# Attention scores from two products of 128 rows per sub-head, with keys stacked high and low and queries doubled, in place of three products of 64 rows

## The reference, cut to what matters

```
q, k, v = xn @ wq.T, xn @ wk.T, xn @ wv.T      # q, k: 8 heads x 2 sub-heads of 64; v: 8 heads of 64
scores  = q @ k.T / 8                          # for each of the 16 sub-heads, 1024 x 1024, causal
attn    = softmax(scores)                      # fp32
attn    = attn[first sub-head] - lmbda * attn[second sub-head]
out     = attn @ v                             # then a root-mean-square norm, and @ wo.T
```

## Time and profile before

| | |
|---|---|
| median of 3 runs | 3775.64 us (3774.65 to 3775.76) |
| the profiled execution | 3770.78 us |
| its span, first to last instruction | 3769.0 us |
| mean granted TensorE clock | 0.94 |
| PE busy | 3183.8 us, 84% |
| DVE / ACT / POOL busy | 1951.8 / 1364.2 / 1859.7 us |

### The profile page before, as it was taken

The page is one execution under the profiler, slowest core; times in us unless marked ns, Lnnn a source line. Parts: engine busy times, 40 slices in busy tenths (PEclk is TensorE's granted clock), DMA queues, the critical chain, the costliest instruction groups (busy, mean ns, idle before and its releaser), DMA issues. The chain is left out here.

```text
span 3769.0 us, 46728 instructions
## 1 busy us (share of the span) xinstructions
PE 3183.8 (84%) x16049; PEld 2443.1 (65%) x16049; DVE 1951.8 (52%) x3951; ACT 1364.2 (36%) x2989; POOL 1859.7 (49%) x1707
## 2 busy tenths in 40 slices
PE   2899999899999979999989999995888983088776
PEld 0677777677777767777767777773776762044443
DVE  6355556645565655655664556565544655811110
ACT  2344444344444424444443444443323321022221
POOL 3256667646576645765773657654222241033333
PEclk9899999999999999999999999997998986589998
DMA  5211111321111141110123111103121111099897
GB/s 156 83 37 43 40 37 43 106 71 45 31 43 45 40 134 40 40 48 29 40 84 98 43 37 40 42 21 121 54 70 67 58 64 60 18 266 246 240 245 177
DMA packets 251183, 301.99 MB, mean 80 GB/s; under 512 B 19664, under 2 KB 168016, under 8 KB 250320
## 3 DMA queue, kind: packets, MB, share of 16 engines
q1 hardware_dynamic: 236624, 263.49, 22.3%
q0 software_dynamic: 14336, 35.66, 4.5%
HBM read 233.46 MB, written 65.57 MB: 79 GB/s over the span
## 5 line engine op out<-in xcount | busy, mean ns | idle before, releaser
L799 ACT ACTIVATE probs<-score_ps,neg_max 128x640 f32<-128x640 f32 (+7 forms) x512 | 374.4, 738 | 363.0 <-DVE neg_max L660 362.5
L690 POOL TENSOR_TENSOR probs<-probs 128x512 f32<-128x512 f32 (+3 forms) x384 | 383.4, 1013 | 10.7
L685 POOL TENSOR_SCALAR probs<-probs,comb 128x512 f32<-128x512 f32 (+3 forms) x384 | 230.0, 607 | 309.2 <-DVE comb L596 301.3
L660 DVE TENSOR_REDUCE neg_max<-score_ps 128x2 f32<-128x256 f32 (+7 forms) x256 | 346.5, 1353 | 58.9 <-PE score_ps L915 55.2
L694 POOL TENSOR_TENSOR out_root<-out_root,neg_half 128x16 f32<-128x16 f32 x128 | 371.8, 2907 | 5.7 <-DVE out_root L630 5.7
L552 DVE TENSOR_TENSOR layer_sum<-product_ps,layer_sum 128x512 f32<-128x512 f32 x384 | 262.4, 684 | 44.7 <-PE product_ps L61 41.6
L912 PE MATMUL score_ps<-keys_all,queries_all 64*128 64x512 f32 (+3 forms) x2304 | 277.2, 363 | 0.0
L539 DVE TENSOR_TENSOR attT<-turn_ps,attT 128x512 fp32r<-128x512 f32 (+3 forms) x384 | 211.6, 551 | 84.5 <-ACT attT L720 84.3
L720 ACT ACTIVATE attT<-turn_ps 128x512 fp32r<-128x512 f32 (+3 forms) x384 | 188.2, 490 | 142.8 <-PE turn_ps L825 142.8
L912 PEld LDWEIGHTS score_ps<-keys_all,queries_all 64*128 64x128 f32 x2304 | 187.8, 185 | 74.0 <-issue 44.7
L59 PE MATMUL product_ps<-xT_hi,w_up 128*128 128x512 f32 x512 | 211.6, 413 | 28.3 <-DVE queries_all L559 20.2
(11 more groups left out here) (248 smaller groups left out, 7676.3 us busy)
## 6 DMA issues: line engine op xcount, KB each, us to landing
e_gate_up<-in_w_gate_dram SPq DMA_DIRECT2D x64, 384.0 KB, 4.0
e_gate_up<-in_w_up_dram SPq DMA_DIRECT2D x64, 384.0 KB, 5.4
e_down<-in_w_down_dram SPq DMA_DIRECT2D x64, 384.0 KB, 6.8
w_stage<-in_wqk_dram SPq DMA_DIRECT2D x64, 256.0 KB, 3.1
w_stage<-in_w1T_dram SPq DMA_DIRECT2D x64, 256.0 KB, 2.6
w_stage<-in_w3T_dram SPq DMA_DIRECT2D x64, 256.0 KB, 2.7
values_by_head<-hidden_split SPq DMA_DIRECT2D x32, 512.0 KB, 3.2
w_stage<-w_transformed SPq DMA_DIRECT2D x64, 256.0 KB, 2.7
```

The lines of the kernel that those rows point to most:

```text
L660: dve.tensor_reduce(nmax[:, i % 2, :], score_tile(i % NT), AX.X, ALU.max, negate=True)\
L685: pool.tensor_scalar(PR[:, r, 1, c], PR[:, r, 1, c], comb[:, i % 4:i % 4 + 1], 1.0, ALU.mult, ALU.mult)\
L690: pool.tensor_tensor(PR[:, r, 0, c], PR[:, r, 0, c], PR[:, r, 1, c], ALU.add).then_inc(s_comb, 1)
L799: act.activation(PR[:, i % 2, q, 0:(j + 1) * P], score_tile(j)[:, q, :], ACT.Exp, bias=nmax[:, i % 2, q:q + 1], accum_out=sums[:, i % 16, ...
```

## The change

K holds, per head and sub-head, 128 rows: the sub-head's 64 rows of high parts on one half of the partitions and its low parts on the other half. Q holds, per sub-head, the high and the low part of the queries, each on both halves of the partitions. A product of 128 rows then gives query part x (high key + low key) at once, and two of them (high and low query) make the scores of a sub-head; low x low, which was left out before, comes with it. So a chunk of keys takes 4 matmuls of 128 rows in place of 6 of 64.

`proj_high` and `proj_low` write each half of the partitions by an instruction of its own (64 rows each), since the halves go to different places. The other half of Q is filled by DMA, from SBUF to SBUF: `double_queries`, two transfers of 256 KB for each half of a head's tokens, issued by SP when `proj_low` has freed the bank; `scores` waits for them (semaphores z_q_double0 and z_q_double1) at j = 0 and j = 4.

Q has room for one head only. So the queries of a head are projected later (`proj_at`): quarters 0, 1 and 2 of head h+1 in steps 2, 4 and 6 of head h, and quarter 3 in step 0 of head h+1 itself. In slot 12 there are three quarters instead of four. The weights wv can no longer be put into Q during head 7: their four pieces move from steps 3 and 4 of head 7 to slots 0 and 1.

```diff
--- before.py
+++ after.py
@@ -278,6 +278,7 @@
         s_vld = [sem("z_v_load0"), sem("z_v_load1")]
         s_gbf, s_gbfree, s_ph, s_tanh = sem("z_gb_filled"), sem("z_gb_free"), sem("z_proj_high"), sem("z_tanh")
         s_hh, s_hl = sem("z_hidden_high"), sem("z_hidden_low")
+        s_qd = [sem("z_q_double0"), sem("z_q_double1")]
         s_scf, s_max, s_exp = sem("z_sc_filled"), sem("z_max"), sem("z_exp")
         s_rs, s_cc, s_scaled, s_comb = sem("z_recip"), sem("z_comb_factor"), sem("z_scaled"), sem("z_comb")
         s_ttf, s_tth, s_ttfree = sem("z_tt_filled"), sem("z_tt_high"), sem("z_tt_free")
@@ -311,7 +312,10 @@
 
         def proj_at(i):
 
-            return (i // NT + 1, i % NT // 2) if 0 <= i < STEPS - NT and i % 2 == 0 else None
+            if not 0 <= i < STEPS or i % 2:
+                return None
+            h, q = (i // NT, 3) if i % NT == 0 else (i // NT + 1, i % NT // 2 - 1)
+            return (h, q) if h < HEADS else None
 
         def pair_at(i):
 
@@ -328,6 +332,8 @@
                 got += {0: [("wv", 0, 0, 0), ("wv", 0, 1, 0)], 1: [("wv", 0, 2, 0), ("wv", 0, 3, 0)],
                         2: [("qk", 0, 0, 1)], 3: [("qk", 0, 0, 0)], 4: [("w1", 0, 0, 0)], 5: [("w3", 0, 0, 0)],
                         6: [("w1", 0, 0, 1)]}.get(s, [])
+            if hb and s in (0, 1):
+                got += [("wv", hb, 2 * s, 0), ("wv", hb, 2 * s + 1, 0)]
             if hb is not None and s == HEAD_SLOTS - 1:
                 got.append(("qk", hb, 1, 1))
             if b is not None and i < STEPS:
@@ -340,8 +346,6 @@
                     got.append(("qk", *after, 0))
                 if s8 in (1, 2):
                     got.append(("w2", b, 2 * h + s8 - 1, 0))
-                if s8 in (3, 4) and h == HEADS - 1 and more:
-                    got += [("wv", b + 1, 2 * (s8 - 3), 0), ("wv", b + 1, 2 * (s8 - 3) + 1, 0)]
                 if s8 == 5 and more:
                     got.append(("w1", *after, 0))
                 if s8 == 6 and more:
@@ -378,7 +382,7 @@
                 if pair_at(i):
                     gb["W", b, i] = len(gb)
             if hb is not None and s == HEAD_SLOTS - 1:
-                for q in range(4):
+                for q in range(3):
                     gb["P", hb, 0, q] = len(gb)
             for v in pieces_at(b, i, hb, s):
                 piece[v] = len(order)
@@ -410,6 +414,9 @@
 
         def wv_part(part):
             return (K, Q)[part][:, 0, :, :].rearrange("p a n -> p (a n)").rearrange("p (k n) -> p k n", k=KT)
+
+        def query_quarter(b, h, half):
+            return gb["P", b, h, 2 * half + 1] + 1, slice(half * D, (half + 1) * D)
 
         def place(part, v):
             kind, _, a, c = v
@@ -472,6 +479,13 @@
                 def load_values(b, h):
                     sp.dma_start(Vh[:, h % 2, :, :].rearrange("p t n -> p (t n)").bitcast(F32), v_d[b, h])\
                       .then_inc(s_vld[h % 2], 16)
+
+                def double_queries(b, h, half):
+                    done, c = query_quarter(b, h, half)
+                    sp.wait_ge(s_gbfree, done)
+                    for q, here, there in ((0, lo64, hi64), (1, hi64, lo64)):
+                        v = Q[:, q, :, c].bitcast(F32)
+                        sp.dma_start(v[there], v[here]).then_inc(s_qd[half], 16)
 
                 for t in range(2):
                     load_x(0, t)
@@ -512,6 +526,10 @@
                         h = (i + 5) // NT
                         sp.wait_ge(s_pvf, b * GROUPS + 4 * (h - 2) + 4)
                         load_values(b, h)
+                    if b is not None and i < STEPS and proj_at(i - 1) and proj_at(i - 1)[1] % 2:
+                        double_queries(b, proj_at(i - 1)[0], proj_at(i - 1)[1] // 2)
+                    if hb is not None and s == HEAD_SLOTS - 1:
+                        double_queries(hb, 0, 0)
                     for v in pieces_at(b, i, hb, s):
                         load_piece(piece[v] + 3)
                 for t in range(NT):
@@ -555,11 +573,14 @@
                 def proj_low(b, h, q):
                     c, r = slice(q // 2 * D, (q // 2 + 1) * D), h % 2
                     dve.wait_ge(s_ph, (b * HEADS + h) * 4 + q + 1)
-                    if q % 2:
-                        ins = dve.scalar_tensor_tensor(Q[:, r, 1, c], gbank("P", b, h, q), 0.125,
-                                                       Q[:, r, 0, c].bitcast(F32), ALU.mult, ALU.subtract)
-                    else:
-                        ins = dve.tensor_tensor(K[:, r, 1, c], gbank("P", b, h, q), K[:, r, 0, c].bitcast(F32), ALU.subtract)
+                    raw = gbank("P", b, h, q)
+                    for sub, here, there in ((0, lo64, hi64), (1, hi64, lo64)):
+                        if q % 2:
+                            ins = dve.scalar_tensor_tensor(Q[here, sub, 1, c], raw[here, :], 0.125, Q[here, sub, 0, c].bitcast(F32),
+                                                           ALU.mult, ALU.subtract)
+                        else:
+                            ins = dve.tensor_tensor(K[there, r, sub, c], raw[here, :], K[here, r, sub, c].bitcast(F32),
+                                                    ALU.subtract)
                     ins.then_inc(s_gbfree, 1)
 
                 for b, i, hb, s in phases():
@@ -730,10 +751,12 @@
                 def proj_high(b, h, q):
                     c, r = slice(q // 2 * D, (q // 2 + 1) * D), h % 2
                     act.wait_ge(s_gbf, gb["P", b, h, q] + 1)
-                    if q % 2:
-                        ins = act.activation(Q[:, r, 0, c], gbank("P", b, h, q), ACT.Copy, scale=0.125)
-                    else:
-                        ins = act.activation(K[:, r, 0, c], gbank("P", b, h, q), ACT.Copy)
+                    raw = gbank("P", b, h, q)
+                    for sub, here in ((0, lo64), (1, hi64)):
+                        if q % 2:
+                            ins = act.activation(Q[here, sub, 0, c], raw[here, :], ACT.Copy, scale=0.125)
+                        else:
+                            ins = act.activation(K[here, r, sub, c], raw[here, :], ACT.Copy)
                     ins.then_inc(s_ph, 1)
 
                 def piece_high(v):
@@ -743,7 +766,7 @@
                     if before in gb:
                         act.wait_ge(s_gbf, gb[before] + 1)
                     if v[0] == "wv" and v[1]:
-                        act.wait_ge(s_scf, (v[1] - 1) * STEPS + STEPS - NT)
+                        act.wait_ge(s_scf, v[1] * STEPS)
                     act.activation(place(0, v), staged(v), ACT.Copy).then_inc(s_wh, 1)
 
                 for b, i, hb, s in phases():
@@ -898,7 +921,8 @@
                     hd, j = divmod(i, NT)
                     n, r = (j + 1) * P, hd % 2
                     if j in (0, 4):
-                        pe.wait_ge(s_gbfree, gb["P", b, hd, 1 if j == 0 else 3] + 1)
+                        pe.wait_ge(s_gbfree, gb["P", b, hd, j // 2] + 1)
+                        pe.wait_ge(s_qd[j // 4], 32 * (b * HEADS + hd + 1))
                     done = b * STEPS + i - (1 if 1 <= j < 4 else 0)
                     if done:
                         pe.wait_ge(s_exp, 2 * done)
@@ -907,10 +931,10 @@
                         pe.wait_ge(s_vlo, (b + 1) * NT)
                     for c0 in range(0, n, D):
                         w = min(D, n - c0)
-                        for m, (qp, kp) in enumerate(((0, 0), (1, 0), (0, 1))):
-                            for q, rows in enumerate((lo64, hi64)):
-                                pe.matmul(score_bank(q, j, c0)[:, 0:w], Q[rows, r, qp, j * P:(j + 1) * P],
-                                          K[rows, r, kp, c0:c0 + w], start=(m == 0), stop=(m == 2 and c0 + w < n))
+                        for q in range(2):
+                            for part in range(2):
+                                pe.matmul(score_bank(q, j, c0)[:, 0:w], Q[:, q, part, j * P:(j + 1) * P],
+                                          K[:, r, q, c0:c0 + w], start=(part == 0), stop=(part == 1 and c0 + w < n))
                     for q in range(2):
                         ins = pe.matmul(score_bank(q, j, c0)[:, w - P:w], identb[:, :], mask[:, :], start=False, stop=True)
                     ins.then_inc(s_scf, 1)
```

## The result

| | before | after |
|---|---|---|
| median, same chip | 3775.14 us | 3938.32 us (3928.33 to 3941.26) |
| ratio, 95% interval | | 1.0441 [1.0424, 1.0458] |
| profiled execution, span | 3770.78, 3769.0 us | 3936.04, 3934.3 us |

The account below looks back on a forecast made before the run. The prediction took PE's own order in layer 0 as the bound: its score time and its waits. Terms of -11 + 55 + 16 + 2 + 2 + 7 = +71 us put the median at 3847 us, range 3812 to 3893.

Parts of the forecast that it names:

- B: Projection's readers at pair heads: two instructions each free the bank 1.14 us later, all on PE at 48 places; +55 us.
- C: Row maximum at j = 7: DVE runs without idle time, so the 1.14 us delay reaches PE's attT wait; +16 us.
- F: The clock: waits grown beyond 2.2 us halve the granted clock behind a quarter of 24, 1.2 us each; +7 us.
- A: Scores on PE: four full-height products per chunk replace six half-row ones, whose ends of 0.30 us per block vanish; -11 us.
- D: Start of a batch: PE reaches the first scores sooner and waits 0.6 us for the query copies, four times; +2 us.
- E: Pieces of wv moved to slots 0 and 1 on POOL: the next batch's first norm starts 0.9 us late, three times; +2 us.
- not slower: Rival: 64-row reader instructions take half the time of 128-row ones, so the readers cost nothing; 3768 us, chance 0.04.
- ends stay: Rival: the 0.30 us per score block is no matter of half rows and remains; 3924 us, chance 0.06.
- weights: Rival: weights no longer load under products, so each score product pays 185 ns; 4131 us, chance 0.01.
- copies late: Rival: SP reaches the query doubling so late that PE waits 1 us at each of 60; 3907 us, chance 0.03.
- waits absorbed: Rival: PE's other waits in the same step shrink by half of the readers' cost at pair heads; 3819 us, chance 0.09.

Follow-up runs that it names:

- b_split: Kernel before with only the projection's readers (proj_high on ACT, proj_low on DVE) split into two instructions of 64 rows each; 3926.2 us, 1.0417.
- b_scores: Kernel before with only the score products changed to two of full height per sub-head, on the old buffers (scores are other numbers); 3776.0 us, 1.0015.
- d_ms: b_split with one small DVE instruction, the mean square of out_root, moved to POOL; 3874.7 us, 1.0286 against before.
- b_ms: Kernel before with the small mean-square instruction on out_root moved from DVE to POOL; 3770.3 us, 1.0002.
- b_sched: Kernel before with only the moved steps: projection quarters one slot later, wv's pieces in slots 0 and 1; 3771.1 us, 1.0002.
- c_fill: b_split with groups of 18 small bf16 products added on PE in its waits, results unused; 3877.6 us, 1.0279 against before.
- c_dve: Kernel before with only DVE's half of the reader split (proj_low in two 64-row instructions, proj_high whole); 3839.7 us, 1.0178.
- c_act: Kernel before with only ACT's half of the reader split (proj_high in two 64-row instructions, proj_low whole); 3804.7 us, 1.0094.
- a_pipe: Changed kernel with ACT signalling after each 64-row instruction and DVE waiting only for the one it needs; 3849.0 us, 1.0200 against before.

## Why the prediction was wrong, by its own steps

The readers were priced at 78 us and cost 157. Of b_split's 153.5 us in the steps, B has 62 (forecast 55), C's three steps 24 (16 with step 7, which shows no loss), places for which the forecast had no term 18, and the low clock 48 (7). So F was mis-sized most, and C's mechanism failed.

*A* (-11): the mechanism was right, the ends went with the half rows; +6.5 measured, which is not shown to differ from 0 but is not -11 (interval -0.4 to +12). The term is mis-sized at the small products: the estimate was 0.07 us for 128 columns, the trace after has 0.12 between them. With 8 such in a head, 8 x 0.05 x 32 = 12 us, and the gain is gone. By b_scores' trace steps 0 to 62 are 8.8 us longer, and 7.3 of these are idle time, most of it ahead of pv_ps and turn_ps, which no term had.

*B* (+55): 48 x 1.29 = 62. The places and the mechanism were right. I priced the second instruction by the distance to the next start of other instructions (0.53, 0.61); two readers of one bank stand 0.60 and 0.70 apart, their whole durations.

*C* (+16): this step failed. The claim was that DVE runs from the low part to the row maximum without idle time, so that a shift of 1.14 passes through as 1.14. It holds for the queue and not for the durations: `comb` gives 0.39 of the shift back, and the small instruction on out_root adds 1.17 by its stall behind POOL. Steps 15, 31 and 47 lost 2.03 each in b_split, and the steps behind them another 9.5 in all. That stalls of the small instruction are what makes the difference is shown by d_ms (51 us less, the low clock that follows included) with b_ms (nothing) beside it; how the 2.03 divides is read from the traces.

*D and E* (+2, +2): a wait of 1.33 to 1.40 instead of 0.6 at the batch's start, some 5 us. The profile puts three of the four down to "issue" and one to DVE; that it is the copies which end them is not shown. E is within b_sched's 1.7.

*F* (+7): mis-sized by far, 48 us by c_fill and the step sums. The bound of 29 was of one stretch for each of 24 waits at 1.2 us; there were 27, at 1.8. The share of 1/4 came from waits between batches; in b_split 19 of the 23 waits of 2.35 to 2.42 us have a stretch behind them, five of the 13 of 1.88 to 1.90 at w_up, and three of the eight of 2.01 to 2.08 ahead of turn_ps. So waits under the 2.2 us of which the prediction spoke have them too, and the length of the wait alone does not tell where one begins.

The rivals: *not slower* fell with B; *ends stay* and *weights* fell with b_scores; *copies late*: the score products of after wait only at the four batches' starts (5.4 us in all); *waits absorbed* is the opposite of what happened. *C* and *F* feed each other: behind a step with a low stretch DVE meets POOL's next sum. In b_split the small instruction takes 1.23 to 1.29 us and the wait of turn_ps 2.01 to 2.08 in the eight of steps 16, 32 and 48 that have a stretch ahead of them, and 0.37 and 1.15 in the four that have none. In c_dve the wait is 2.01 to 2.07 in five of the seven with a stretch ahead, 0.96 and 1.04 in the other two, and 1.16 to 1.19 in the five without. The clock and the stalls together are why half of the delay costs a fifth (c_act) and all of it 157.

## What to carry to other kernels

Splitting these instructions by partitions doubled their time (each of 64 rows takes as long as the one of 128 did, 0.59 us on ACT and 0.69 on DVE); ask of each reader of a PSUM bank what waits for that bank, and let the second engine begin on the first half when it is written (a_pipe: 89 us by moving two lines). If a change delays an engine, its instructions do not keep their durations: look at what the neighbour engine does at the new time. And when several waits grow at once, bound the sum by a case where each also brings the low clock, not by a share.

## What the runs showed of the hardware

- Small products of full height are not as cheap as their columns: 128 columns start 0.12 us apart in the score blocks, 256 also 0.12, 384 0.18, 512 0.23.
- A DVE `tensor_scalar` of 16 columns from and to SBUF, begun during POOL's `tensor_tensor` of 512 columns, took up to 1.29 us instead of 0.17, until POOL's instruction was over (b_split; before has 20 of over 0.5 us too, and b_ms, without them, is no faster).
- A stall can also go away when an instruction comes later: `comb` takes 0.61 us in before and 0.22 in c_act, 0.59 later in its step.
- Work of no use on PE (some 71 us of bf16 products in its waits) made the kernel 49 us faster: granted clock 1.00 where b_split has 92 us at half.
